# One comparison for four edge tiles: one-hots of a graph sum from two 16-bit tensors

## What is computed

```python
xn = layernorm(x)                                # x: 6250 nodes x 256, float32
neigh_sum = segment_sum(xn[src], dst, 6250)      # 200000 edges, sorted by dst
deg = segment_sum(ones, dst, 6250)
h = concat([xn, neigh_sum / max(deg, 1)]) @ W + b
g = relu(h);  g = g / max(norm(g), 1e-12)
x = x + g + linear_attention(xn)                 # 8 heads of 32
x = x + moe(layernorm(x))                        # 8 experts, top 2, dense: every expert on every node
```

## Time and profile before

| | |
|---|---|
| median of 3 runs | 2122.65 us (2122.04 to 2126.42) |
| span of the profiled execution, first to last instruction | 2123.1 us |
| GpSimd busy | 1542.4 us, 73% |
| TensorE matmul busy | 1659.0 us, 78% |
| VectorE busy | 1257.9 us, 59% |
| ScalarE busy | 592.5 us, 28% |
| gathers | 1,568 of 956 ns mean |
| one-hots | 1,560 of 276 ns and 8 of 251 ns mean |

### The profile page before, as it was taken

The page is one execution under the profiler, slowest core; times in us unless marked ns, Lnnn a source line. Parts: engine busy times, 40 slices in busy tenths (PEclk is TensorE's granted clock), DMA queues, the critical chain, the costliest instruction groups (busy, mean ns, idle before and its releaser), DMA issues.

```text
span 2123.1 us, 39942 instructions
## 1 busy us (share of the span) xinstructions
PE 1659.0 (78%) x9865; PEld 1214.8 (57%) x9865; DVE 1257.9 (59%) x5773; ACT 592.5 (28%) x1473; POOL 1542.4 (73%) x1595
## 2 busy tenths in 40 slices
PE   0388766698888888788888778888788888778888
PEld 0144434476666656566666566666565656556567
DVE  8522232476666656666666656666666666656565
ACT  5233311133222223232223222323232323222223
POOL 5577777777777777777777777777777777777770
PEclk9999966799999999999999999999999999999999
DMA  7478777544343434344434343444343434343340
GB/s 244 152 220 256 239 213 205 150 114 119 112 120 110 121 113 120 113 120 113 120 111 120 111 122 113 119 112 120 111 121 112 120 113 120 111 118 113 112 118 13
DMA packets 150450, 280.53 MB, mean 132 GB/s; under 512 B 31374, under 2 KB 93118, under 8 KB 150206
## 3 DMA queue, kind: packets, MB, share of 16 engines
q0 software_dynamic: 75264, 205.62, 34.6%
q1 hardware_dynamic: 74942, 72.17, 10.5%
HBM read 245.58 MB, written 32.09 MB: 131 GB/s over the span
## 4 chain that ended last, share of the span: by engine, by line
POOL 51%; issue 18%; PE 17%; DMA 6%; DVE 5%; ACT 1%; POOLq 0%; DVEq 0%; ACTq 0%; SPq 0%
POOL sb_ring L577 51%; DMA sb_ring<-xn_table,sb_idx_now 5%; PE ps_expert L802 3%; PE ps_hidden L792 3%; PE ps_zone L624 2%; PE ps_zone L626 1%; PE ps_proj L737 1%; PE ps_proj L677 1%; PE ps_proj L759 1%; PE ps_hidden L677 1%; PE ps_proj L762 1%; DMA xn_transposed<-sb_stage 1%; DVE sb_stats L1074 1%; PE ps_turned L633 1%; DVE sb_small L1118 1%
## 5 line engine op out<-in xcount | busy, mean ns | idle before, releaser
L577 POOL DMA_INDIRECT sb_ring<-xn_table,sb_idx_now x1568 | 1498.5, 956 | 487.3 <-issue 459.8
L624 PE MATMUL ps_zone<-sb_ring,sb_onehot 128*128 128x256 f16 x1568 | 416.3, 284 | 303.7 <-DMA sb_ring<-xn_table,sb_idx_now 242.3
L969 ACT ACTIVATE sb_stage<-ps_hidden,sb_b_col 128x128 f32<-128x128 f32 x784 | 245.5, 364 | 796.9 <-PE ps_hidden L792 796.3
L792 PE MATMUL ps_hidden<-sb_arena 128*128 128x128 f32 x3136 | 440.9, 286 | 0.0
L802 PE MATMUL ps_expert<-sb_arena,sb_stage 128*128 128x256 f32 x1568 | 427.5, 398 | 1.4 <-DVE sb_arena L1378 1.2
L624 PEld LDWEIGHTS ps_zone<-sb_ring,sb_onehot 128*128 128x128 f16 x1568 | 155.3, 99 | 469.9 <-issue 220.2
L626 PE MATMUL ps_zone<-sb_ring,sb_onehot 128*128 128x257 f16 x1568 | 415.5, 283 | 0.0
L792 PEld LDWEIGHTS ps_hidden<-sb_arena 128*128 128x128 f32 x3136 | 397.8, 198 | 26.9 <-issue 17.1
L1148 DVE TENSOR_SCALAR sb_onehot<-sb_iota,sb_rel_now 128x128 f16<-128x128 f16 x1560 | 360.6, 276 | 13.6 <-PE ps_zone L626 1.5
L1378 DVE SCALAR_TENSOR_TENSOR sb_arena<-ps_expert,sb_small,sb_arena 128x256 f32<-128x256 f32 x392 | 188.7, 481 | 279.1 <-PE ps_expert L802 263.2
L802 PEld LDWEIGHTS ps_expert<-sb_arena,sb_stage 128*128 128x128 f32 x1568 | 283.6, 202 | 26.2 <-issue 2.2
(11 more groups left out here) (135 smaller groups left out, 1748.3 us busy)
## 6 DMA issues: line engine op xcount, KB each, us to landing
sb_ring<-xn_table,sb_idx_now POOLq DMA_INDIRECT x1568, 2.8
keys_values<-sb_stage SPq DMA_DIRECT2D x49, 256.0 KB, 2.7
sb_arena<-keys_values SPq DMA_DIRECT2D x96, 128.0 KB, 3.0
sb_arena<-x SPq DMA_DIRECT2D x7, 896.0 KB, 11.6
xn_table<-sb_stage SPq DMA_DIRECT2D x7, 896.0 KB, 4.7
xn_transposed<-sb_stage SPq DMA_DIRECT2D x49, 128.0 KB
sb_arena<-xn_transposed SPq DMA_DIRECT2D x49, 128.0 KB
sb_arena<-x SPq DMA_DIRECT2D x49, 128.0 KB
```

The source lines that it names most:

```text
L577: pool.indirect_dma_start(ring3[:, place, 0:2 * D], None, table, bass.IndirectOffsetOnAxis(tile_idx, 0)).then_inc(signal, 16)
L624: pe.matmul(bank_[:, 0:D], oh, rows[:, 0:D], start=first, stop=False, skip_group_check=True)
L792: mm = pe.matmul(hidden[e % 2][:, j * P:(j + 1) * P], w1_sb[:, e, c, j * P:(j + 1) * P], halves(tokens_t[b.par])[:, c, :], start=c == 0, s ...
L969: ins = act.activation(halves(act_h[e % len(act_h)])[:, j, :], hidden[e % 2][:, j * P:(j + 1) * P], ACT.Gelu, bias=b1_col[:, e * KC + j:e ...
```

## The change

`rel` and `rel_now` become 16-bit and hold each value twice, side by side. `place_edges` computes in float32 in a third stretch of the ring's space (`rel_wide`) and copies the result, doubled and cast, into `rel` with one more instruction. Four tiles' one-hots are made by one `tensor_tensor` whose inputs are both tensors: `iota16`, read again for each tile, and the four pairs, each read 64 times. It waits until the last of its four places is free, and counts `onehot_made` up by four. Where a step's tiles hold an index that four divides, the step issues that batch.

```diff
+OH_BATCH = 4
...
-        rel = sb("rel", TILES)
-        rel_now = sb("rel_now", TURN_TILES)
+        rel = sb("rel", 2 * TILES, F16)
+        rel_now = sb("rel_now", 2 * TURN_TILES, F16)
...
+        rel_wide = ring[:, :].bitcast(F32)[:, 2 * TILES:3 * TILES]
+        rel_pairs = rel[:, :].rearrange("p (t c) -> p t c", c=2)
...
-                dve.tensor_tensor(rel[:, :], dst_i, rel[:, :].bitcast(I32), ALU.subtract).then_inc(far_chain, 1)
+                dve.tensor_tensor(rel_wide, dst_i, rel_wide.bitcast(I32), ALU.subtract).then_inc(far_chain, 1)
...
                 dve.tensor_reduce(far_max, far[:, :], AX.X, ALU.max).then_inc(far_reduced, 1)
                 yield
+                dve.tensor_copy(rel_pairs, rel_wide.unsqueeze(2).to_broadcast([P, TILES, 2])).then_inc(far_chain, 1)
+                yield
...
             dve.tensor_copy(iota16[:, :], cst[:, C_IOTA:C_IOTA + P]).then_inc(far_chain, 1)
             dve.wait_ge(far_reduced, 1)
+            dve.wait_ge(far_chain, 6)
             dve.memset(ring3[:, :, 2 * D:2 * D + 1], 1.0).then_inc(cleared, 1)
...
-            def tile_onehot(tile, rel_col, place):
-                dve.wait_ge(tiles_used, tile + RING - OH_RING + 1)
-                make_onehot(place, rel_col).then_inc(onehot_made, 1)
+            def tile_onehots(tile, pairs, place):
+
+                dve.wait_ge(tiles_used, tile + OH_BATCH + RING - OH_RING)
+                dve.tensor_tensor(
+                    onehot3[:, place:place + OH_BATCH, :].rearrange("p t (c two) -> p t c two", two=2),
+                    iota16[:, :].rearrange("p (c two) -> p c two", two=2).unsqueeze(1).to_broadcast(
+                        [P, OH_BATCH, P // 2, 2]),
+                    pairs.rearrange("p (t two) -> p t two", two=2).unsqueeze(2).to_broadcast(
+                        [P, OH_BATCH, P // 2, 2]),
+                    ALU.is_equal).then_inc(onehot_made, OH_BATCH)
+
+            def pairs_of(tensor, j):
+
+                return tensor[:, 2 * j:2 * (j + OH_BATCH)]
+
+            def batches(tiles):
+
+                return [j for j in tiles if j % OH_BATCH == 0]
...
-                dve.tensor_copy(rel_now[:, first:first + tiles],
-                                rel[:, bass.ds(tile0 + first + LEAD, tiles)]).then_inc(rel_copied, 1)
+                dve.tensor_copy(rel_now[:, 2 * first:2 * (first + tiles)].rearrange("p (t c) -> p t c", c=2),
+                                rel_pairs[:, bass.ds(tile0 + first + LEAD, tiles), :]).then_inc(rel_copied, 1)
...
-                for j in tiles:
+                for j in batches(tiles):
                     if not isinstance(tile0, int) or tile0 + j + LEAD < TILES:
-                        tile_onehot(tile0 + j + LEAD, rel_now[:, j:j + 1], (j + LEAD) % OH_RING)
+                        tile_onehots(tile0 + j + LEAD, pairs_of(rel_now, j), (j + LEAD) % OH_RING)
                         yield
```

More of the change, by code:

```diff
@@ L88 @@
 assert TILES % TURN_TILES == 0 and MAIN_TILE % RING == 0
+assert all(n % OH_BATCH == 0 for n in (LEAD, OH_RING, B1_TILES, B2_TILES, B2_FIRST, ZONE_TILES, TURN_TILES, LAST_TILES))
 C_EYE = P
@@ L561, in _ @@
         def _(pool):
-            pool.iota(rel[:, :].bitcast(I32), [[ZONE_NODES, ZONES], [0, ZONE_TILES]], base=-ZONE_BACK,
+            pool.iota(rel_wide.bitcast(I32), [[ZONE_NODES, ZONES], [0, ZONE_TILES]], base=-ZONE_BACK,
                       channel_multiplier=0).then_inc(base_made, 1)
@@ L1085, in place_edges @@
                 dve.wait_ge(base_made, 1)
-                dve.tensor_tensor(rel[:, :], dst_i, rel[:, :].bitcast(I32), ALU.subtract).then_inc(far_chain, 1)
+                dve.tensor_tensor(rel_wide, dst_i, rel_wide.bitcast(I32), ALU.subtract).then_inc(far_chain, 1)
                 yield
                 dve.wait_ge(far_chain, 1)
-                dve.tensor_scalar(below, rel[:, :], 0.0, None, ALU.is_lt).then_inc(far_chain, 1)
+                dve.tensor_scalar(below, rel_wide, 0.0, None, ALU.is_lt).then_inc(far_chain, 1)
                 yield
                 dve.wait_ge(far_chain, 2)
-                dve.scalar_tensor_tensor(out=outside, in0=rel[:, :], scalar=float(P - 1), in1=below,
+                dve.scalar_tensor_tensor(out=outside, in0=rel_wide, scalar=float(P - 1), in1=below,
                                          op0=ALU.is_gt, op1=ALU.add).then_inc(far_chain, 1)
@@ L1144, in _ @@
             dve.wait_ge(sums_cleared, 1)
-            dve.wait_ge(far_chain, 5)
+            dve.wait_ge(far_chain, 6)
             def make_onehot(place, rel_col):
@@ L1188, in copy_rel @@
                 dve.wait_ge(onehot_made, tile0 + first + LEAD)
-                dve.tensor_copy(rel_now[:, first:first + tiles],
-                                rel[:, bass.ds(tile0 + first + LEAD, tiles)]).then_inc(rel_copied, 1)
+                dve.tensor_copy(rel_now[:, 2 * first:2 * (first + tiles)].rearrange("p (t c) -> p t c", c=2),
+                                rel_pairs[:, bass.ds(tile0 + first + LEAD, tiles), :]).then_inc(rel_copied, 1)
                 dve.wait_ge(rel_copied, copies)
-            for t in range(LEAD):
-                tile_onehot(t, rel[:, t:t + 1], t)
+            for t in batches(range(LEAD)):
+                tile_onehots(t, pairs_of(rel, t), t)
             for n in range(ROW_BUFS):
@@ L1207, in _ @@
                 for k in range(B1_BLOCKS):
-                    for j in b1_tiles(k):
-                        tile_onehot(i * B1_TILES + j + LEAD, rel_now[:, j:j + 1], (j + LEAD) % OH_RING)
+                    for j in batches(b1_tiles(k)):
+                        tile_onehots(i * B1_TILES + j + LEAD, pairs_of(rel_now, j), (j + LEAD) % OH_RING)
                     max_keys(i * B1_BLOCKS + k, k)
@@ L1249, in _ @@
                     shift_keys(i * B2_BLOCKS + k, i * (B2_BLOCKS // KV_BUFS) + k // KV_BUFS, k % KV_BUFS)
-                    for j in b2_tiles(k):
-                        tile_onehot(tile0 + j + LEAD, rel_now[:, j:j + 1], (j + LEAD) % OH_RING)
+                    for j in batches(b2_tiles(k)):
+                        tile_onehots(tile0 + j + LEAD, pairs_of(rel_now, j), (j + LEAD) % OH_RING)
                     for z in zones_ended(b2_tiles(k)):
```

## The result

| | median | lowest to highest | runs |
|---|---|---|---|
| before | 2123.39 us | 2120.93 to 2126.42 | 20 |
| after | 2127.08 us | 2124.93 to 2128.76 | 20 |

The change makes the kernel slower by a little: the ratio is 1.0017, 95% interval 1.0010 to 1.0024, or +3.7 us. Measured again later (e8), it was 1.0025 [1.0016, 1.0034], +4.8 us. Forecast were +10.3 us. The direction was right and the time lies inside the stated range (2118 to 2148), at the lower end of the forecast's own, 2127. But the size was more than twice too large, and the kernel before measured 0.7 us more here than the 2122.65 from which the forecast was added up.

A forecast was written before the change was run, and what follows sets the result against it. GpSimd's chain of gathers was taken as the bound. Comparisons +11.3, one-hots -2.5, start +1.8 and tail -0.3 gave +10.3 us on 2122.65 us, so 2133 us; stated range 2118 to 2148, the forecast's own 2127 to 2145.

The forecast's parts named there:

- What bounds the kernel: GpSimd's gathers, one every 1.25 us, set the time; VectorE's one-hots are not in the sum.
- The mechanism, two SBUF inputs hold a gather up: A gather starting inside a VectorE operation with two SBUF inputs waits until about 0.13 us before that operation's end.
- The comparison at 425 ns: Each four-tile comparison on VectorE was taken to last 425 ns, two columns to a cycle; upper bound 0.69 us.
- Rival A: The comparison runs at one column a cycle and makes gathers wait 44 us in all: 2166 us; chance 12%.
- The start, +1.8 us: The doubled copy before the first gather shifts the whole rest by 1.8 us.
- The wait, priced at nothing: A batch's stricter wait for its four places on VectorE costs no time, covered by GpSimd's chain of gathers.
- The tail, −0.3 us: In the last 77 us, five batches in place of 20 one-hots gain 0.3 us.
- so a share of 0.216 of them meets a gather: Comparisons meet gathers by chance, 29 ns each; 388 cost 11.3 us, bounds near 3 and 23 us.
- the one-hots' −2.5: Removing the one-input one-hots, which sometimes hold up gathers, gains 2.5 us, bounds 0 and 3.6.
- B: Rival: batches fall between gather starts and cost some 3 to 5 us, giving 2124 to 2127 us; chance 15%.
- C: Rival: the chain's two-input operations (L1309, L1321, L1323) move off gather starts, their 10.0 us go down, kernel faster; chance 9%.
- A mean of 956 or less: A mean gather time of 956 ns or less would show the forecast wrong; about 962 would show it right.

The follow-up runs named there:

- e6: e3 with an idle one-input statistics operation of 420 ns behind each group of four one-hots, 392 times: 2122.56 us, 1.0000 of the kernel before.
- e4: The kernel after, with the comparison reading one stored copy 128 times instead of the pair 64 times: 2162.05 us, 1.0185 of the kernel before.
- e5: e3 with an idle float32 addition of two SBUF tensors, 425 ns, behind each group of four one-hots: 2151.16 us, 1.0135 of the kernel before.
- e1: The kernel before with only the doubled copy added, written to a place nobody reads: 2124.20 us, 1.0009 of the kernel before.
- e3: The kernel before with one-hots grouped in fours at the change's places and with its wait, still one-input operations: 2121.96 us, 0.9997.
- e13: The kernel before itself, run and traced once more: 2121.71 us, 0.9993.
- e16: The kernel after with each step's batches of comparisons issued behind the whole chain, not inside it: 2129.21 us, 1.0028 of the kernel before.
- e7: The kernel after with a second, equal comparison into scratch ahead of each: 2142.48 us, 1.0091 of the kernel before.

## Why the prediction was right, and where it failed

- **What bounds the kernel:** right. Saved VectorE work came back as TensorE's wait for gathers; e6 adds 164 us of VectorE work for nothing; e4 and e5 show that lengthened gathers are paid in full (+35.9 and +29.9 us of gathers, +39.6, of which 2.1 to 2.4 are the start, and +28.7 us of time).
- **The mechanism, two SBUF inputs hold a gather up:** right, by e5 against e6 and by L1378. It is not the whole: some operations with one tensor input hold gathers up too, by the same accounting the one-hots 1.6 to 2.1 us and in the kernel after L1357 and L1331, float32 from SBUF to SBUF, 0.6 and 0.5 us in six gathers each.
- **The comparison at 425 ns:** right, 421. Rival A did not occur, and e4 shows what it would have been.
- **The start, +1.8 us:** right; the first gather was 1.9 to 2.1 us later in the traces. e1's times have 1.8, within 0 to 3.8.
- **The wait, priced at nothing:** right for the time, by e3 and by the waits; VectorE does wait 19.7 us for TensorE before batches, 18 times, under the gathers' cover.
- **The tail, −0.3 us:** from the last gather's start to the end are 53.1 us after and in e13, 54.3 in the first trace before; nothing to be seen.
- **The step that failed:** "so a share of 0.216 of them meets a gather, which waits half of 0.27: 29 ns each, and 388 x 29 ns = 11.3 us". With the one-hots' −2.5, the gathers' term was +8.8 us. It was about +2.4: the comparisons cost 6.1 to 8.3 us, and against them stand not only the one-hots (1.6 to 2.1 us, inside its bounds) but the sum of squares' 3.5 us, which the sum did not have; the other lines together moved by +1.0 us in one trace and -0.3 in the other. The estimate took every operation's place as independent of the gathers'. It is not: a gather holds up what runs on VectorE and so sets the place of what follows, and an operation inserted into a chain moves every later one. The prediction had both halves as rivals. The mechanism of B (kind places) took 3 to 5 us off the comparisons' price, and that of C (the chain's operations move off the gathers' starts) took off 3.5 more, for one line of the three that it named. Each was priced as a case of its own against the forecast, where both happened in part and together, on top of a full start. The two measurements, +3.7 and +4.8 us, lie at the upper end of B's +1.4 to +4.4 and just above it, not at the forecast. That the time still fell at the forecast's lower end is in part luck, by the 0.7 us that the kernel before measured more.
- **VectorE busy 195 us less:** wrong, 83. The one-hots' busy time was taken off whole, though much of it lay beside other operations.
- **A mean of 956 or less** was named as a sign against the forecast, and it was one.

## What to carry to other kernels

Where GpSimd issues a gather for every tile and sets the time, count VectorE's operations with two SBUF tensor inputs first, not its busy time (some with one input cost a little too): replacing many one-input operations by fewer two-input ones can make a kernel slower though it frees 80 us of the engine. A chance of meeting gives such a price only to within a factor of two or so: against 11.3 us by the formula stood 6.1, 8.3 and 7.8 (e16), against 23 stood 23.9 (e7), against 44 stood 41.5 (e4), and against 11 in e5, behind one-hots, 23.0 and the rows. Look in the trace at what stands right behind an operation that a gather has held up, for those places repeat, and doubling the suspected operation or exchanging it for a one-input one of the same length measures it. What paid here was the opposite edit: the sum of squares from a one-input operation, 2117.99 us, 0.9975 [0.9965, 0.9986] of the kernel before.

## What the runs showed of the hardware beyond this

- The hold works both ways. A gather makes L1308 and its like, float32 with one tensor input, wait to end 1.06 us after the gather's start (13 to 21 of 49 blocks). The Trainium skill, page "SBUF — State Buffer", section "SBUF: two separate sides", says that whichever starts first has the shared ports for the whole instruction. For comparisons the runs agree on who wins, down to 20 ns, but not on the whole instruction: a gather gets in 0.13 us before the recorded end of a comparison. For a float32 operation with one tensor input they don't agree on who wins either: in 7 blocks of e13, L1334 starts 0.13 us before a gather, the gather takes its plain 0.95 us, and L1334 takes 0.45 us in place of 0.41.
- Float32 operations with two inputs that follow each other without a pause hold a gather up together (the 16-bit comparisons of e7 don't): 1.50 us in place of 0.95 above, and 1.79 us across three of them elsewhere in e5 (its timeline):

```profile
276.83 1.09 DVE L1255 TENSOR_TENSOR sb_arena<-sb_arena,sb_stage 128x256 f32<-128x256 f32 x3
...
276.95 1.79 POOL L580 DMA_INDIRECT sb_ring<-xn_table,sb_idx_now  x1 [0.30 <-issue]
```

- Two executions of the same kernel before differ by 2.1 us in their gathers (1498.5 and 1496.4), as much as the change's own effect on them. A single trace of each kernel would have given the wrong account; it took the timed runs and four more traces without the comparison to see it.
